# A graph transformer on one core: the products that prepare a sorted part are spread over the program's slots and set between other products

## The reference

```
xn  = layernorm(x) * ln1_g + ln1_b
xp  = xn + xn @ Wpos + bpos + deg * Wdeg + bdeg
q, k, v = xp @ Wq + bq, xp @ Wk + bk, xp @ Wv + bv      # 8 heads of 16
att = clip(sum_d(q[dst] * k[src]) / sqrt(16), -50, 50)
alpha = softmax of att over the edges of one destination
x   = x + (segment_sum(v[src] * alpha, dst) @ Wo + bo)
x   = x + gelu(layernorm(x) @ W1 + b1) @ W2 + b2        # FF = 512
```

## Time and profile before

| | |
|---|---|
| runs shown, us | 3673.75, 3679.43, 3686.6 (median 3679.43) |
| the profiled execution | 3681.54 us, its span 3679.6 us |
| mean granted TensorE clock | 0.904 |
| busy: TensorE products, weight loads | 3094.9 us (84%), 2455.6 us (67%) |
| busy: VectorE, GpSimd, ScalarE | 2917.6 us (79%), 2567.7 us (70%), 1812.1 us (49%) |
| instructions | 74225 |

### The profile page before, as it was taken

One profiled execution on the slowest core, in us unless ns is written; L12 is line 12 of the kernel. 1 busy time (PEld: TensorE's weight loads), 2 busy tenths in 40 slices (PEclk: granted clock), 3 DMA queues, 4 the chain that ended last, 5 costly groups with the idle time before them and its releaser, 6 DMA issues.

```text
span 3679.6 us, 74225 instructions
## 1 busy us (share of the span) xinstructions
PE 3094.9 (84%) x25656; PEld 2455.6 (67%) x25656; DVE 2917.6 (79%) x6187; ACT 1812.1 (49%) x4404; POOL 2567.7 (70%) x2470
## 2 busy tenths in 40 slices
PE   3993589898898998998997588888888888989896
PEld 3762467677777776776775466766677676767675
DVE  8986578888888898888886468777887777878886
ACT  1331135454555554555564345555555555655565
POOL 1006777777777777777775577777777777777774
PEclk7675679999999999999999799999999999999997
DMA  3006345555555555555553455555565555555552
GB/s 86 23 26 187 112 140 164 157 165 156 161 175 160 174 161 157 172 153 162 158 174 107 134 160 173 171 175 165 166 181 171 170 171 173 172 173 165 166 180 71
DMA packets 426827, 558.32 MB, mean 152 GB/s; under 512 B 78430, under 2 KB 345020, under 8 KB 426256
## 3 DMA queue, kind: packets, MB, share of 16 engines
q0 software_dynamic: 117504, 321.02, 29.8%
q1 hardware_dynamic: 301442, 225.28, 20.1%
q10 hardware_dynamic: 7506, 7.20, 0.6%
HBM read 527.79 MB, written 25.44 MB: 150 GB/s over the span
## 4 chain that ended last, share of the span: by engine, by line
POOL 34%; PE 25%; DVE 21%; issue 13%; ACT 4%; DMA 1%; DVEq 1%; POOLq 0%; SPq 0%
POOL kv_ring L1969 26%; POOL arena L1969 8%; PE psum L958 4%; DVE scratch L1680 3%; DVE scratch L1704 3%; PE psum L1032 3%; DVE att L1689 3%; PE psum L1015 2%; PE psum L1069 2%; PE psum L1048 2%; PE psum L999 2%; DVE work L1384 2%; DVE kv_ring L1401 2%; PE psum L834 1%; DVE arena L1731 1%
## 5 line engine op out<-in xcount | busy, mean ns | idle before, releaser
L1969 POOL DMA_INDIRECT kv_ring<-kv_table,src_idx x1840 | 1922.9, 1045 | 634.3 <-issue 557.3
L1234 ACT ACTIVATE scratch<-psum 128x512 f32<-128x512 f32 (+1 forms) x1228 | 698.4, 569 | 501.8 <-PE psum L968 338.6
L1969 POOL DMA_INDIRECT arena<-kv_table,src_idx x608 | 626.4, 1030 | 189.5 <-issue 184.6
L958 PE MATMUL psum<-arena 128*128 128x256 f32 x2156 | 628.0, 411 | 111.7 <-ACT scratch L1234 111.4
L958 PEld LDWEIGHTS psum<-arena 128*128 128x128 f32 x2156 | 378.1, 195 | 236.0 <-ACT scratch L1234 144.5
L1689 DVE TENSOR_REDUCE att<-scratch 128x64 f32<-128x1024 f32 (+1 forms) x460 | 535.4, 1164 | 0.2
L1680 DVE TENSOR_TENSOR scratch<-psum,kv_ring 128x1024 f32<-128x1024 f32 x230 | 280.6, 1220 | 285.7 <-DMA kv_ring<-kv_table,src_idx 228.1
L1245 ACT COPY arena<-psum 128x512 f32<-128x512 f32 x616 | 326.4, 531 | 297.0 <-PE psum L958 287.7
L1269 ACT ACTIVATE scratch<-att 128x64 f32<-128x64 f32 (+1 forms) x460 | 117.2, 255 | 685.9 <-DVE att L1695 681.6
L999 PEld LDWEIGHTS psum<-q_win,scratch 64*128 64x128 f32 x4896 | 326.0, 203 | 177.3 <-issue 172.4
L999 PE MATMUL psum<-q_win,scratch 64*128 64x128 f32 x4896 | 387.4, 302 | 67.2 <-DVE scratch L1680 59.4
(11 more groups left out here) (252 smaller groups left out, 4681.1 us busy)
## 6 DMA issues: line engine op xcount, KB each, us to landing
arena<-kv_table SPq DMA_DIRECT2D x154, 896.0 KB
kv_ring<-kv_table,src_idx POOLq DMA_INDIRECT x1840
q_win<-q_table SPq DMA_DIRECT2D x612, 32.0 KB
work<-kv_table SPq DMA_DIRECT2D x98, 128.0 KB
q_win<-q_table SPq DMA_DIRECT2D x154, 64.0 KB
arena<-kv_table,src_idx POOLq DMA_INDIRECT x608
work<-q_table SPq DMA_DIRECT2D x98, 64.0 KB
kv_table<-work SPq DMA_DIRECT2D x49, 128.0 KB
```

The lines of the kernel that those rows point to most:

```text
L958: mm = e.matmul(to[:, t % 2 * 2 * D:(t % 2 + 1) * 2 * D], hot_source[:, t * P:(t + 1) * P], source_rows[m % 2][:, t, :], start=True, stop= ...
L1234: e.activation(to[:, at:at + width], apart[k % FILL_BANKS][:, 0:width], ACT.Relu, bias=1.0, scale=-1.0).then_inc(apart_read, 1)
L1969: e.indirect_dma_start(kv[m % RING_KV][:, t, :], None, kv_table[l], bass.IndirectOffsetOnAxis(ap=src_idx[:, c * T + t:c * T + t + 1], axis ...
```

## The change

Fills are placed by a search: each in the emptier slot of a small range (`place`), the later one where two are equal. The result for a block v: source 0 in slot 2v - 8 (before: 2v - 7), source 1 in 2v - 7 (as before), rows 0 to 3 in 2v - 7, 2v - 6, 2v - 5, 2v - 4 (before: 2v - 5 twice, 2v - 4 twice); turns in 2v - 4 and hots in 2v + 1 as before. The most fills in a slot stay four; slots with four go from 137 to 2 in layer 0 and from 144 to 23 in layer 1.

Inside a slot TensorE takes one fill ahead of each half, one behind them, then one behind each banked node or sort product, then the rest. ScalarE evicts two ahead of the exponential as before; the others now come behind the node steps, or ahead of the GELU table's load, and between and behind the two halves of the GELU. `one_hots_made` counts the fills issued so far (`issued`) in place of `fills_before`.

```diff
@@ -161,15 +161,33 @@
 
     def fills(self):
 
-
-        fills = {-1: [("turn", u, h) for u in range(2) for h in range(self.parts_of(u))]}
-        for u in range(self.nu):
-            ahead = [("source", u + 4, h) for h in range(2) if self.is_block(u + 4)]
-            turn = [("turn", u + 2, h) for h in range(self.parts_of(u + 2))] if u + 2 < self.nu else []
-            hot = [("hot", u, h) for h in range(self.parts_of(u))]
-            rows = [[("rows", u + (3 if i < 2 else 2), i)] if self.is_block(u + (3 if i < 2 else 2)) else [] for i in range(4)]
-            fills[2 * u] = turn[:1] + rows[2] + turn[1:] + rows[3]
-            fills[2 * u + 1] = hot[:1] + rows[0] + hot[1:] + rows[1] + ahead
+        fills = {slot: [] for slot in range(-1, 2 * self.nu + 2)}
+
+        def place(first, last, of):
+
+            first, last = max(first, -1), max(last, -1)
+            slot = min(range(first, last + 1), key=lambda at: (len(fills[at]), -at))
+            fills[slot].append(of)
+            return slot
+
+        for u in range(2):
+            for h in range(self.parts_of(u)):
+                fills[-1].append(("turn", u, h))
+        for v in range(self.nu + 4):
+            if self.is_block(v):
+                done = [place(2 * v - 9 + h, 2 * v - 8 + h, ("source", v, h)) for h in range(2)]
+                at = 0
+                for i in range(4):
+                    at = place(max(at, done[i // 2], 2 * v - 8 + i), max(at, 2 * v - 7 + i), ("rows", v, i))
+            if 2 <= v < self.nu:
+                at = 0
+                for h in range(self.parts_of(v)):
+                    at = place(max(at, 2 * v - 5), 2 * v - 4, ("turn", v, h))
+            u = v - 3
+            if 0 <= u < self.nu:
+                at = 0
+                for h in range(self.parts_of(u)):
+                    at = place(max(at, 2 * u), 2 * u + 1, ("hot", u, h))
         return fills
@@ -273,7 +291,7 @@
 
 
 FILLS = [layer.fills() for layer in LAYERS]
-FILL_ORDER = [(l, *f) for l in range(L) for u in range(-1, 2 * LAYERS[l].nu) for f in FILLS[l][u]]
+FILL_ORDER = [(l, *f) for l in range(L) for u in range(-1, 2 * LAYERS[l].nu + 2) for f in FILLS[l][u]]
 FILL_AT = {f: k for k, f in enumerate(FILL_ORDER)}
@@ -596,11 +614,7 @@
             l, u = layer_of(n)
             return FILL_AT[l, what, u, h]
 
-        def fills_before(l, slot):
-
-            made = FILLS[l][-1] if slot < 0 else [
-                f for s in range(-1, slot + 1) for f in FILLS[l].get(s, [])[:1 if s == slot else None]]
-            return max(FILL_AT[l, *f] for f in made)
+        issued = [0]
 
         def unit(l, u):
             return LAYERS[l].unit0 + u
@@ -933,9 +947,10 @@
                 e.wait_ge(apart_read, k + 1 - FILL_BANKS)
             return apart[k % FILL_BANKS]
 
-        def one_hots_made(e, k, since):
-
-            if since < k + FILL_BANKS:
+        def one_hots_made(e, k):
+
+            assert k < issued[0]
+            if issued[0] <= k + FILL_BANKS:
                 e.wait_ge(apart_read, k + 1)
 
         def source_by_edge(e, n, h):
@@ -978,6 +993,8 @@
 
         def tensor_fill(e, l, what, u, h):
             n = unit(l, u)
+            assert FILL_ORDER[issued[0]] == (l, what, u, h)
+            issued[0] += 1
             if what == "turn":
                 place_by_edge(e, n, h)
             elif what == "hot":
@@ -987,10 +1004,15 @@
             else:
                 gather_rows(e, n, h)
 
+        def next_fill(e, l, fills):
+
+            for fill_of in itertools.islice(fills, 1):
+                tensor_fill(e, l, *fill_of)
+
         def spread_chunk(e, l, u):
 
             n = unit(l, u)
-            one_hots_made(e, fill(n, "turn", 0), fills_before(l, 2 * u - 2))
+            one_hots_made(e, fill(n, "turn", 0))
             e.wait_ge(q_in[n % QUERIES], 16 * q_loads[n])
             if n >= 1:
                 e.wait_ge(prod_ready, 2 * n)
@@ -1005,7 +1027,7 @@
 
             n = unit(l, u)
 
-            one_hots_made(e, fill(n, "hot", 0), fills_before(l, 2 * u + 3))
+            one_hots_made(e, fill(n, "hot", 0))
             e.wait_ge(msg_ready, n + 1)
             bank_free(e, bank_use[l, u, "edges"], True)
             to = edge_sum(l, u)
@@ -1023,7 +1045,7 @@
                 if h == 0:
                     spread_chunk(e, l, u)
                 return
-            one_hots_made(e, fill(n, "turn", h), fills_before(l, 2 * u - 2))
+            one_hots_made(e, fill(n, "turn", h))
             e.wait_ge(q_in[n % QUERIES], 16 * q_loads[n])
             if f >= 2:
                 e.wait_ge(prod_ready, f - 1)
@@ -1040,7 +1062,7 @@
                     sum_chunk(e, l, u)
                 return
             if h == 0:
-                one_hots_made(e, fill(n, "hot", 1), fills_before(l, 2 * u + 3))
+                one_hots_made(e, fill(n, "hot", 1))
                 e.wait_ge(msg_ready, n + 1)
                 bank_free(e, bank_use[l, u, "edges"], True)
             last = LAYERS[l].tiles_of(u) - 1
@@ -1145,20 +1167,25 @@
                     spread_queries(e, l, 0, h)
                 for slot in range(slots_of(l)):
                     u = slot // 2
-                    fills = FILLS[l].get(slot, [])
+                    fills = iter(FILLS[l].get(slot, []))
                     for h in range(2):
-                        for fill_of in fills[h:h + 1]:
-                            tensor_fill(e, l, *fill_of)
+                        next_fill(e, l, fills)
                         if slot % 2 == 0 and u + 1 < LAYERS[l].nu:
                             spread_queries(e, l, u + 1, h)
                         if slot % 2 == 1 and 1 <= u <= LAYERS[l].nu:
                             sum_edges(e, l, u - 1, h)
-                    for fill_of in fills[2:]:
-                        tensor_fill(e, l, *fill_of)
+                    next_fill(e, l, fills)
                     for j, k in at(slots, slot):
                         node_tensor(e, l, j, k, True)
+                        if k in BANKED:
+                            next_fill(e, l, fills)
                     for s, k in at(SORTS[l], slot):
                         sort_tensor(e, s, k)
+                        if k in SORT_BANKED:
+                            next_fill(e, l, fills)
+                    for fill_of in fills:
+                        tensor_fill(e, l, *fill_of)
+
 
 
         def early_scalar(e, i):
@@ -1308,6 +1335,17 @@
         cleared_by = [[sum(len(clear_spans(i, j)) for i in range(l) for j in range(LAYERS[i].jb))
                        + sum(len(clear_spans(l, j)) for j in range(n)) for n in range(LAYERS[l].jb + 1)] for l in range(L)]
 
+        def gelu_half(e, l, j, h):
+
+            g, ps = ws(l, j)[2], node_bank(bank_use[l, j, "ff_in"])
+            if h == 0:
+                e.wait_ge(node_mm["ff_in"], nth(l, j, ""))
+            for f in range(h * FC // 2, (h + 1) * FC // 2):
+                a = e.activation(g[:, f * P:(f + 1) * P], ps[:, f * P:(f + 1) * P], ACT.Gelu, bias=cols[:, l, 8 + f:9 + f])
+            if h == 1:
+                a.then_inc(gelu_ready, 1)
+                e.preload_act_table_set(TABLES)
+
         def node_scalar(e, l, j, k, held):
             row, col, g, qkv, own, tiny = ws(l, j)
             i = nth(l, j, "")
@@ -1336,12 +1374,8 @@
 
                 e.preload_act_table_set(GELU_TABLES)
             elif k == GELU:
-                e.wait_ge(node_mm["ff_in"], i)
-                for f in range(FC):
-                    a = e.activation(g[:, f * P:(f + 1) * P], ps("ff_in")[:, f * P:(f + 1) * P], ACT.Gelu,
-                                     bias=cols[:, l, 8 + f:9 + f])
-                a.then_inc(gelu_ready, 1)
-                e.preload_act_table_set(TABLES)
+                for h in range(2):
+                    gelu_half(e, l, j, h)
             elif k == 24:
                 node_scale(e, l, j, 1)
             elif k == 28:
@@ -1349,6 +1383,11 @@
                 e.activation(col, ps("next_t")[:, 0:P], ACT.Identity, scale=cols[:, l + 1, 2:3],
                              bias=cols[:, l + 1, 3:4]).then_inc(next_ready, 1)
 
+        def next_scalar_fill(e, l, fills):
+
+            for fill_of in itertools.islice(fills, 1):
+                scalar_fill(e, l, *fill_of)
+
         def scalar_edges(e):
             for l in range(L):
                 slots = node_steps(l)
@@ -1361,15 +1400,24 @@
                     scalar_fill(e, l, *fill_of)
                 for slot in range(slots_of(l)):
                     u = slot // 2
-                    fills = FILLS[l].get(slot, [])
-                    for fill_of in fills[:2]:
-                        scalar_fill(e, l, *fill_of)
+                    fills = iter(FILLS[l].get(slot, []))
+                    next_scalar_fill(e, l, fills)
+                    next_scalar_fill(e, l, fills)
                     if slot % 2 == 0 and u < LAYERS[l].nu:
                         make_exp(e, l, u)
-                    for fill_of in fills[2:]:
```

(14 more changed lines are left out.)

## The result

The changed kernel takes **3698.18 us** (median of 12 runs, 3693.47 to 3710.62) against 3680.83 us for the kernel before (12 runs, 3673.75 to 3696.85). The ratio is **1.0047, with a 95% interval of 1.0032 to 1.0063**: 17 us slower. The prediction said 3673 and no change, with a range to 3692. It was wrong. The profiled execution after takes 3695.82 us (span 3693.9) against 3681.54, 14.3 us more.

The account below looks back on a forecast made before the run. GpSimd's gathers were taken as the bound. The profiled 3681.5 us less 6 for message waits, with 0 for gather pace and other pieces, gave 3675.5; the runs' median, 2.1 lower, made it 3673, range 3650 to 3692.

Parts of the forecast that it names:

- The ground: Whole execution: GpSimd's gathers, a 1.25 us cycle and never free, bound the kernel; the compute engines' work is hidden.
- Burst removal: TensorE before row products: most of 111 us of waits for ScalarE's evictions goes, none of it from the end.
- 35 us in that stretch: TensorE, 727 to 1809 us: the 111 us spread as 0.24 us per unit over 144 units.
- Waits for messages: GpSimd before gathers: 11 waits of 9.3 us hold 6.0 us of loss, all taken as gone; bounds 0 and -6.
- 3 us or less: Sign: GpSimd's waits for message products fall from 9.3 us to this.
- layer 0's gathers per 400 us: Sign: these stay at 291 to 298; 300 and more would mean gathers speed up.
- the gathers' pace: Both rows of gathers: same products in the same order, so 0 change; bounds -36 and +10 us.
- Between the layers and behind: Pieces between and after the two rows of gathers: 45 and 44 us, both to stay.
- The slower rival: ScalarE's late evictions put compute engines behind GpSimd, 727 to 1809 us: 23 us more, 3702; chance 0.16.
- The faster rival: Layer 0's gathers speed up as message products start at a set moment: up to 36 us, half taken, 3655; chance 0.30.
- DVE waits for gathers grow from 278: Sign: VectorE's total waits for gathers grow from 278 us.
- VectorE's waits for the block queries: VectorE waiting on TensorE, 94.4 us: should shrink with two or three fills to a slot; argued against late evictions.

Follow-up runs that it names:

- layer1_only: Kernel before with the whole change in layer 1 alone, layer 0 as before: 3704.69 us, ratio 1.0053 to the kernel before.
- placement_only: Kernel before with fills in the new slots but the old order inside a slot, both layers: 3700.12 us, ratio 1.0044 to the kernel before.
- layer0_only: Kernel before with the whole change in layer 0 alone, layer 1 as before: 3682.25 us, ratio 0.9993 to the kernel before.
- inslot_only: Kernel before with fills in the old slots but the new order inside a slot, both layers: 3681.46 us, ratio 0.9994 to the kernel before.
- before_pad_third: Kernel before plus a 128x512 memset ahead of every layer 1 message product, on a slow chip: 5451.90 us, ratio 0.9768 to the kernel before.
- before_pad_again: Kernel before plus a 128x512 memset ahead of every layer 1 message product, another run on a slow chip: 5573.66 us, ratio 0.9795.

## Why the prediction was wrong

**The ground held.** The gathers bound the kernel before and after: 0.30 us of issue ahead of each, 5.9 us of waits for messages. TensorE's and VectorE's gains stayed hidden.

**Burst removal: right for the rows, too high for TensorE.** "I take most of the 111 us as removed from TensorE, and none of it from the end": the wait before the rows went from 111.4 to 11.2 us, all waits for evictions by 63 us, and there was no gain. The prediction also spread the 111 us evenly over the units, "35 us in that stretch", from 727 to 1809 us. The trace of before has 12.4 us there and 94.7 us in layer 1.

**Waits for messages: right in sign, half the size.** I took 6.0 us of loss as gone. By the same working 5.9 - 10 x 0.30 = 2.9 us are left of it, a gain of 3.1. Of the tests, "3 us or less" failed at 5.9; layer 0's gathers per 400 us stayed within 291 to 298, as forecast.

**The failed step is the second one of what reaches the end, "the gathers' pace. The same products run in the same order, so I take 0", with +10 as its upper bound.** It measured +17 us in layer 1 (stretch 98.3 to 114.9) and +1 in layer 0. That the same products run in the same order was true and beside the point: a product's price is its rest at the next gather's start, and this hangs on the microsecond at which VectorE comes to it. I had seen that this could move and had no way to price it, and drew the bound on the upper side from nothing ("with no row against it, +10, a third of that"). A bound was there in the rows: the 460 products' stretch is 191 us of the 227 us of all stretch before, and could have been 0 or, at 1.2 us for each, some 550. Against such ends 17 us is a small shift, and a bound of +10 was too tight.

**Between the layers and behind: right within 3 us.** 47.9 us between, after 45.0; 44 us to the end of the span in both.

**The slower rival came near the number, 3702 for 3698, by the wrong mechanism: that was luck.** It needed the compute engines behind GpSimd and waits over 20 us. The waits fell. **The faster rival had the right mechanism and the wrong sign.** It said that a product behind a VectorE that waited for its gather starts at a set moment. In layer 1 before, the 55 products behind such a wait have 0.23 us of stretch each, the other 178 have 0.45. But VectorE wasn't caught up oftener there: 52 such products after, and their stretch went up to 0.35, that of the others to 0.50. The test "DVE waits for gathers grow from 278" came out true in total:

```profile
DVE scratch L1728 <- DMA kv_ring<-kv_table,src_idx: 271.3, 72, 17.8
DVE scratch L1728 <- PE psum L1054: 115.4, 66, 5.5
...
DVE scratch L1728 <- DMA arena<-kv_table,src_idx: 51.7, 16, 6.2
```

323 us, and was no sign of a gain: a longer gather makes VectorE wait too. Nor did VectorE's waits for the block queries shrink, as I had argued: 94.4 us to 115.4 here. In layer 1 (2200 to 3400 us) they went from 23.6 to 41.5 us, and they go with the loss in the other kernels: 36.5 us in layer1_only and 35.9 in placement_only, against 25.8 in layer0_only and 14.6 in inslot_only. This may be what moves the products, since the earlier source fill stands between the halves of a block's queries on TensorE. That it is this fill was argued from the order and not tested.

**What stays open**: which moved fill shifts layer 1's products, and why layer 0's, under the same change, stay where they are. One row hints at the second: of the 111 us of burst waits that the change takes away, layer 0 had 16.7 us and layer 1 94.7, so that TensorE's times moved little in layer 0; no run tests this. Shown are the place of the loss (layer 1's gathers), the part that makes it (the placement), and, by six time lines, that the added time is gathers standing for message products. The six are one execution each.

## What to carry to other kernels

An engine that is never free still has a price per instruction, and others can set it: when the bound is a row of gathers, list what ran on VectorE when the long ones started before costing a re-timing at zero. Of VectorE's three long operations for a unit only the message product, with both operands in SBUF, holds gathers, for 191 us of 3680; most of the other 36 us of stretch ends as far behind other operations with two operands in SBUF, mostly the sort's. Moving hidden work shifted that sum by 17 us to the worse here. To earn some of it one would take an operand of the message product out of SBUF or place it just behind a gather's start; no run here tried either, and on a chip where the gathers bind no version here beat the kernel before by a measurable amount.

## What the runs showed of the hardware that was not expected

A memset holds no gather by itself, but one with a message product right behind it does. In before_pad_third, layer 1:

```profile
3643.12 0.48 DVE L1772 MEMSET pad<- 128x512 f32 x1
3643.21 2.29 POOL L2039 DMA_INDIRECT kv_ring<-kv_table,src_idx  x1 [0.30 <-issue]
3643.52 1.16 DVE L1774 TENSOR_TENSOR scratch<-arena,scratch 128x1024 f32<-128x1024 f32 x1
```

The gather starts inside the memset, 0.31 us ahead of the product, and still ends 0.82 us behind the product's end. In before_pad_again the product waited for ScalarE, and the gather kept its 0.95 us:

```profile
3322.70 0.48 DVE L1772 MEMSET pad<- 128x512 f32 x1
3322.80 0.95 POOL L2039 DMA_INDIRECT arena<-kv_table,src_idx  x1 [0.30 <-issue]
3323.56 1.09 DVE L1774 TENSOR_TENSOR scratch<-arena,scratch 128x896 f32<-128x896 f32 x1 [0.38 <-ACT scratch L1313]
```

In the seven runs with the memset 228 gathers start inside one. In 193 cases the product starts within 0.15 us of the memset's end: 181 of these gathers are stretched, and each ends 0.80 to 0.83 us behind the product's end. In the other 35 it starts later, and none is stretched. My expectation that the memset locks nothing holds for the memset alone. It failed for a product right behind one: the gather then pays for the rest of the memset and for the whole product. Why the product counts from the memset on, and lets a gather in between when a two-operand product stands in the memset's place, is open.

On the slower chips the memset ahead of each of layer 1's messages made the kernel before 2.0 to 2.4% faster, and two runs of a product in its place 0.8%. No row explains either; it stays open.
